# P in bursts of two key tiles, two head groups per PV bank, and another order of the prologue and the tail, in a post-LN transformer block

## The reference

```python
q, k, v = split(reshape(x @ qkv_w.T + qkv_b, heads), 3)
attn = softmax(q @ k.T * SCALE)
x = layernorm(x + (attn @ v) @ fc_w.T + fc_b + x)
h = silu(lin(x, w1, s1)) * lin(x, w2, s2)      # 128 -> 512
h = gelu(lin(h, h1)); h = gelu(lin(h, h2))     # 512 -> 512, exact gelu
x = layernorm(x + lin(h, w3))                  # 512 -> 128
```

## Time and profile before

| | before |
|---|---|
| median of 3 runs | 376.57 us (376.4 to 377.02) |
| profiled execution | 375.58 us, span 373.7 us |
| TensorE busy | 330.5 us (88%) |
| VectorE busy | 251.8 us (67%) |
| ScalarE busy | 249.3 us (67%) |
| GpSimd busy | 157.3 us (42%) |
| DMA | 13.30 MB, mean 36 GB/s |

### The profile page before, as it was taken

How to read it: one execution, slowest core, us unless ns; L and a number is a source line. 1 busy time by engine, 2 the same in 40 slices (tenths; PEclk the granted TensorE clock), 3 DMA queues, 4 the chain that set the end, 5 groups by cost and what they waited for, 6 DMA issues and landing times.

```text
span 373.7 us, 5421 instructions
## 1 busy us (share of the span) xinstructions
PE 330.5 (88%) x1712; PEld 156.5 (42%) x1738; DVE 251.8 (67%) x516; ACT 249.3 (67%) x441; POOL 157.3 (42%) x233
## 2 busy tenths in 40 slices
PE   2947999999999999999999899898997996887992
PEld 1611333222244343344544344363442352366891
DVE  4547878977789877679887678858365710044885
ACT  2605687777667786669667888849867778656440
POOL 9209483300018085004922186727438633308011
PEclk9985999999999999999999999999998998998997
DMA  4643404122130230211031102220000010000001
GB/s 100 191 93 66 150 3 71 38 43 39 16 65 0 36 52 1 44 26 18 3 71 21 25 11 35 43 59 1 0 2 1 1 31 0 1 2 0 2 28 32
DMA packets 21920, 13.30 MB, mean 36 GB/s; under 512 B 6787, under 2 KB 20739, under 8 KB 21891
## 3 DMA queue, kind: packets, MB, share of 16 engines
q1 hardware_dynamic: 21443, 12.53, 16.3%
q10 hardware_dynamic: 448, 0.39, 0.4%
HBM read 5.38 MB, written 1.05 MB: 17 GB/s over the span
## 4 chain that ended last, share of the span: by engine, by line
PE 70%; DVE 7%; ACT 7%; issue 7%; POOL 4%; ACTq 2%; DMA 1%; SPq 1%; POOLq 0%; another core or an unknown queue 0%; DVEq 0%
PE pv_bank L462 16%; PE f_bank L422 16%; PE s_bank L435 13%; PE st_bank L446 13%; DVE negmax L766 4%; ACT prob L628 3%; ACTq L338 2%; PE st_bank L422 2%; PE f_bank L483 2%; PE f_bank L405 2%; DMA res<-in_L_attn_fc_w_dram 1%; PE pv_bank L422 1%; POOL work L955 1%; PE s_bank L422 1%; ACT L628 1%
## 5 line engine op out<-in xcount | busy, mean ns | idle before, releaser
L766 DVE TENSOR_REDUCE negmax<-s_bank 128x1 f32<-128x512 f32 x256 | 167.8, 683 | 54.3 <-PE s_bank L435 52.3
L628 ACT ACTIVATE prob<-st_bank 128x512 f32<-128x512 f32 x256 | 142.0, 596 | 49.3 <-PE st_bank L446 41.4
L435 PE MATMUL s_bank<-stack 125*128 125x512 bf16 x256 | 96.9, 401 | 12.8 <-DVE negmax L766 5.9
L446 PE MATMUL st_bank<-stack 128*128 128x512 bf16 x230 | 82.7, 389 | 4.0 <-ACT prob L628 2.5
L462 PE MATMUL pv_bank<-prob,v_sb 128*32 128x512 f32 x512 | 73.2, 613 | 3.8 <-issue 3.6
L422 PE MATMUL f_bank<-act,hT 128*128 128x512 f32 (+1 forms) x224 | 70.2, 417 | 0.4 <-POOL act L965 0.4
L435 PEld LDWEIGHTS s_bank<-stack 125*128 125x128 bf16 x256 | 23.4, 98 | 78.2 <-DVE negmax L766 41.0
L446 PEld LDWEIGHTS st_bank<-stack 128*128 128x128 bf16 x256 | 23.9, 98 | 56.6 <-ACT prob L628 35.7
L422 PEld LDWEIGHTS f_bank<-act,hT 128*128 128x128 f32 x224 | 41.7, 191 | 8.6 <-issue 0.8
L931 POOL CAST mparts<-negmax 128x16 bf16<-128x16 f32 (+1 forms) x17 | 3.3, 196 | 88.4 <-DVE negmax L766 88.4
L977 POOL TENSOR_TENSOR act<-h_nat,act 128x512 fp32r<-128x512 f32 x24 | 30.4, 1273 | 1.3
(11 more groups left out here) (166 smaller groups left out, 411.2 us busy)
## 6 DMA issues: line engine op xcount, KB each, us to landing
stack<-parts SPq DMA_DIRECT2D x120, 48.0 KB
x_in<-in_L_attn_x_dram SPq DMA_DIRECT2D x4, 256.0 KB, 2.9
h_nat<-in_L_ffn_h_w_dram SPq DMA_DIRECT2D x1, 1024.0 KB, 6.6
work<-in_L_ffn_h_w_dram SPq DMA_DIRECT2D x1, 1024.0 KB, 5.9
x_res<-in_L_attn_x_dram SPq DMA_DIRECT2D x4, 256.0 KB, 2.9
out_dram<-y SPq DMA_DIRECT2D x3, 256.0 KB, 2.3
work<-in_L_ffn_w_w_dram SPq DMA_DIRECT2D x2, 256.0 KB, 5.0
stack<-parts ACTq DMA_DIRECT2D x8, 48.0 KB
```

Of the source, the lines that this page charges most:

```text
L435: nc.tensor.matmul(s_bank[n % NS][:, :], stack[0][0:MROW, h, qt * P:(qt + 1) * P], stack[1][0:MROW, h, :], start=True, stop=True).then_inc ...
L446: last = nc.tensor.matmul(st_bank[n % NST][:, to:to + nq], stack[1][:, h, kt * P:(kt + 1) * P], stack[0][:, h, q0:q0 + nq], start=True, st ...
L628: nc.scalar.activation(prob[:, n % NP, :], st_bank[n % NST][:, :], ACT.Exp, scale=SCALE).then_inc(ev_st, 1)
L766: nc.vector.tensor_reduce(negmax[:, g % 2, col:col + 1], s_bank[n % NS][:, :], AX.X, ALU.max, negate=True).then_inc(ev_s, 1)
```

## The change

- P: `PK = 2`. A P step covers two key tiles: eight matmuls (16 records) after eight T tiles, 34 steps instead of 68. `prob` has 12 slots.
- PV bank: heads are renumbered (`head_of`), V is stored as 18 columns per pair of places, 8 + 8 for two heads and one of ones each, and the P steps of two head groups accumulate in one `pv_bank`. `o`, `or` and `om` occur 8 times instead of 16. The V eviction is two instructions for the two places.
- Prologue: 28 products of zeros on TensorE (`keep_busy`), 22 before the first transpose and 6 after `wq`; the order of loads, transposes and splits is another; `vb` is loaded as one contiguous row to each partition, later; `db` moves from ScalarE to VectorE; the layer scales are loaded as rows and transposed (`hs`).
- `x_res` is `res[0]`; `xres` waits for `x1_ok` of the batch before.
- Tail: batch 2's second Gelu is applied at eviction (`direct`), its `gh` and `gl` move from GpSimd to VectorE; tables are loaded ahead with one-column activations (`ws`, `wg`); the last two units use `act1, act0, act1` where the others use `act0, act1, act0`, and their first split waits for the last H of batch 2 instead of its W.
- All five order texts are rewritten.

```diff
-    VW = 32
+    PO = 2
+    NO = NG // PO
+    VC, VW = PO * (HD + 1), 32
+    PK = 2
-    NP = 8
+    NP = 12
+    def head_of(s):
+        return GH * PO * (s // (GH * PO)) + PO * (s % GH) + s % (GH * PO) // GH
-        x_res = sb("x_res", [P, NT, D], F32)
+        x_res = res[0]
-        v_sb = [sb(f"v_sb{i}", [P, NT, H, VW], F32) for i in range(2)]
+        v_sb = [sb(f"v_sb{i}", [P, NT, H * VC + VW - VC], F32) for i in range(2)]
-        act2 = act0
+        acts = [(act0, act1, act0)] * LT + [(act1, act0, act1)] * TU
+        def direct(u, layer):
+            return u >= LT or (u, layer) == (LT - 1, 1) and True
...
+                elif what == "vb":
+                    sp.dma_start(vb[:, :], qkv_b.partition_broadcast(P)).then_inc(ld_vb, 16)
                 elif what == "xres":
-                    if n:
-                        until_empty(sp, "f", n - 1)
+                    sp.wait_ge(ps_wq, 2)
+                    wait(sp, x1_ok, n)
...
+            def keep_busy(times):
+                for _ in range(times):
+                    nc.tensor.matmul(pv_bank[:, 0:P], wz[:, :], wz[:, :], start=True, stop=True)
+            pe.wait_ge(wz_ok, 1)
+            keep_busy(22)
...
                 elif what == "P":
+                    g, first = n // (NT // PK), PK * n % NT
+                    b, s0, ns = GROUPS[g]
+                    t0 = P_LAST[n] + 1 - PK * ns
                     pe.wait_ge(ev_st, P_LAST[n] + 1)
+                    if first == 0:
+                        wait(pe, ev_pv, NO * b + s0 // (GH * PO))
+                        until_empty(pe, "v", b)
+                    for t in range(t0, t0 + PK * ns):
+                        _, kt, slot = T_TILES[t]
+                        at, of = VW * (slot % GH), VC * head_of(slot)
+                        last = nc.tensor.matmul(pv_bank[at:at + VW, :], v_sb[b % 2][:, kt, of:of + VW], prob[:, t % NP, :],
+                                                start=kt == 0 and slot % (GH * PO) < GH, stop=kt == NT - 1 and slot % (GH * PO) >= GH)
                     last.then_inc(ps_pv, 1)
...
+                elif what in ("ws", "wg"):
+                    nc.scalar.activation(warm[:, :], ident[:, 0:1], (ACT.Silu, ACT.Gelu)[what == "wg"])
...
-                        wait(dve, ps_w3, before(u))
-                    nc.vector.tensor_copy(act0[0][:, k, cols(u)], gate[:, k, cols(u)]).then_inc(hi0 if u < LT else hi0_t, 1)
+                        dve.wait_ge(*((ps_w3, u) if u < LT else (ps_h, 2 * NK * LT)))
+                    nc.vector.tensor_copy(acts[u][0][0][:, k, cols(u)], gate[:, k, cols(u)]).then_inc(hi0 if u < LT else hi0_t, 1)
```

The order texts, their first lines and the parts that matter (a stretch without feed-forward work, and the end of TensorE's and ScalarE's lists):

```diff
 SP_ORDER
-xin lw lh xin zq*2 zk*2 zq zk*2 zq*3 mrow zq*2 lh l3 mrow*2 more xres spread mrow xin spread mrow spread mrow spread mrow xres spread mrow spread mrow
+lw lh xin vb zq*5 zk lh zq zk zq*2 mrow zk*2 l3 xin mrow xin mrow more xres spread mrow spread mrow spread mrow spread xres mrow spread mrow spread
 PE_ORDER
-x:0 wq wf q:1 q:2 v:5 x:0 wt:6 wt:7 v:1 wt:5 wt:2 wt:6 wt:0 S*11 m:1 S*5 T S T S*2 T S P m:2 S*2 T*2 q:0 S*2 P S T*2 q:1 S P S T*2 S wt:2 P S T S T
+x:0 wq wt:1 q:2 q:5 wt:6 v:7 wf wt:0 wt:1 wt:2 wt:5 x:0 v:1 S*11 m:0 S*7 wt:6 S wt:7 S m:1 T*2 S wt:2 S T wt:0 S T S T q:1 S*2 P S*2 T*2 q:2 S T*2 S
...
-S P S*2 T*2 S T S T P S*2 T*2 o:1 S T S T P S a:0 S T S m:2 T f:1 S*2 T*2 P S T*2 q:0 T S T P S T q:2 S T*2 S v:1 S x:0 T S T P T*2 X:2 o:0 S T*2 P S
+T*2 S T S T*2 S T S P S*2 T*2 S T S T m:0 T S T S T S*2 P S*2 T*2 S T S T*2 S T S T S T S T*2 S P S*2 m:2 T*2 S T S T S T*2 S*2 T*2 P S*2 T*2 o:1 S T
...
-T P T*2 H T*2 P T*2 H H:0 T H T H*2 T H:2 T H*2 T H T H:1 H*3 P*2 T o:0 T*3 P T*4 P T*2 H:2 H*2 P H H:1 o:0 H*2 a:3 a:4 H f:5 H:6 H*3 H:7 H*3 f:2 X:0
-A:3 B:4 A:1 B:5 A:6 B:7 A:2 B:0 X:3 W:1 A:4 B:6 A:5 B:2 A:7 W B:3 A:0 B:4 W*2 H:5672 Y:3 H*9 H:0415 H*9 H:6723 H*9 H:0415 H*9 W:6 W*3 W:7 Y:2 W*3 Y:3
+T*2 m:0 Y:2 T*2 P T*2 H:1 o:2 T H T*3 H T*2 P T*2 H H:0 T*2 H*2 T H T H:2 T H T P T*2 H*2 T*2 H:1 H T H T H T P T*7 P o:0 H:2 a:1 a:3 H f:4 H*2 H:5
+H*3 H:6 H X:7 f:0 H*2 H:1 H*3 A:3 B:4 A:2 B:5 W:0 W*2 X:6 W A:7 B:1 A:3 B:2 Y:4 A:0 B:6 A:7 B:5 A:3 B:1 A:0 B:2 H:7360 H*9 H:5127 H*9 H:3604 H*9
 ACT_ORDER
-t e*2 u e*3 o e*2 h e*2 h t h*2 g u e*4 m e*2 t e*4 o w3 e*7 m e*7 h e*2 h e*2 h*2 g o e*12 o h a*2 h*3 g t*8 w3 h*16 w3*2
+m o e*10 h e*3 h e*5 h e*4 h g e*8 wg o a*2 h*4 ws t*2 w3 t*6 wg h*16 w3*2
```

More of the change, by code:

```diff
@@ L8 @@
 SP_ORDER = """
-xin lw lh xin zq*2 zk*2 zq zk*2 zq*3 mrow zq*2 lh l3 mrow*2 more xres spread mrow xin spread mrow spread mrow spread mrow xres spread mrow spread mrow
-spread mrow spread mrow spread xres mrow spread mrow spread mrow spread out xres mrow*3 out*4
+lw lh xin vb zq*5 zk lh zq zk zq*2 mrow zk*2 l3 xin mrow xin mrow more xres spread mrow spread mrow spread mrow spread xres mrow spread mrow spread
+mrow spread mrow spread mrow xres spread mrow spread mrow spread mrow spread out xres mrow*3 out*4
@@ L494, in step @@
                     rows = m_rows(n)
-                    for t in range(m_tiles(n)):
-                        last = nc.tensor.transpose(space("m", n)[:, :].bitcast(BF16)[0:rows, t * P:(t + 1) * P],
-                                                   mparts[:, t * rows:(t + 1) * rows], ident16[:, :])
-                    last.then_inc(ps_mT, 1)
+                    nc.tensor.transpose(space("m", n)[:, :].bitcast(BF16)[0:rows, 0:P], mparts[:, 0:rows], ident16[:, :]).then_inc(ps_mT, 1)
                 elif what == "o":
@@ L588, in step @@
                     last.then_inc(ps_wt, 1)
+                elif what == "hs":
+                    pe.wait_ge(ld_s, 16 * 5)
+                    until_free(pe, "hs", 0)
+                    nc.tensor.transpose(space("hs", 0)[:, 0:4 * NK + 1], hs_nat, ident[0:4 * NK + 1, 0:4 * NK + 1]).then_inc(ps_hs, 1)
                 elif what == "L":
@@ L733, in layernorm @@
                     dve.wait_ge(ps_w3T, u + 1)
+                    wait(dve, y_ok, before(u))
                     nc.vector.tensor_tensor(flat(r), space("Y", u)[:, 0:width(u)], flat(x1_b), ALU.add).then_inc(emptied("Y", u), 1)
```

243 lines of the change are left out of this document (120 added, 123 removed).

## The result

The changed kernel takes 373.56 us (median of 20 runs, 369.84 to 377.01), the kernel before 375.7 beside it (20 runs); the ratio is 0.9921, interval 0.9892 to 0.9951. The forecast was 363.0 with a range of 355.5 to 371.5, so the time is above the range. The profiled execution took 373.0 us, span 371.2, against 375.58 and 373.7: 2.5 us less on the span, where the sum had 13.6.

What follows compares the result with a forecast made beforehand. TensorE was taken as full where feed-forward work runs, a loop of latencies as binding elsewhere; -4.4 - 2.2 - 3.0 + 1.0 - 1.0 - 4.0 = -13.6 us off the 376.57 median gave 363.0 us, range 355.5 to 371.5.

Steps and rivals of the forecast that it cites:

- Bursts, -4.4: P steps: joining 68 into 34 saves 0.20 us at each of 22 pairs where TensorE is full, 4.4 us.
- pairs, -2.2: PV bank: two head groups per bank drop eight times four transposes; five in full stretches at 0.43 save 2.2 us.
- Prologue, -3.0: Start: earlier q, faster clock by fillers and reordered work bring the first S to 20 to 21.5; 3.0 us gained.
- xres, +1.0: Group changes: xres waits for x1_ok, so the next mrow and T may come late; 1.0 us lost in all.
- Wide Gelu, -1.0: Stall of 3.61 us before the P at 314.65: remains, with eight exponentials after it instead of twelve; 1.0 us gained.
- Tail, -4.0: End: direct Gelu, early table loads and exchanged buffers cut last P to first tail H from 21.0 to about 17; 4.0 gained.
- from there on nothing changes: After the first tail H: 128 tail matmuls without gaps, normalization and store stay as before.
- One sign: Tail, expected in the new profile: no table load between the last H and the first gate.
- Rival (a): Full stretches: half of 6.6 us is given back and the tail gains 1.5 only; -7.8, 368.8 us, chance 0.25.
- The hand-worked round: Loop stage without feed-forward work: eight tiles take 6.8 us with a burst against 6.7 now, so 0 booked.
- Rival (c): All 34 bursts: the longer pause is covered nowhere, 0.9 less 0.2 us each, +24; 391 us, chance 0.05.
- rival (d): All bursts: rival (c)'s mechanism at 0.3, so no change; 376.6 us, chance 0.03.

Runs made afterwards that it cites:

- e15: The changed kernel with both the max reductions and the exp activations halved (wrong results); 356.8 us, 0.9528 of the kernel before.
- e16: The kernel before with both the max reductions and the exp activations halved (wrong results); 367.59 us, 0.9817 of the kernel before.
- e14: The kernel before with the paired PV banks alone, eight evictions instead of sixteen; 374.72 us, 1.0004 of the kernel before.
- e13: The changed kernel with one head group per PV bank, sixteen evictions instead of eight; 388.16 us, 1.0345 of the kernel before.
- e3: The changed kernel without the 28 filler products; 372.37 us, 0.9917 of the kernel before.
- e2: The kernel before with its P steps joined in pairs and 12 prob slots, nothing else; 383.8 us, 1.0224 of the kernel before.
- e9: The kernel before with its max reductions halved and the exp scale reduced (wrong results); 371.73 us, 0.9929 of the kernel before.
- e11: The kernel before with its exp activations halved (wrong results); 370.9 us, 0.9868 of the kernel before.
- e18: The changed kernel's code with the old loop and old TensorE prologue order, keeping pairs, fillers and new tail with mended VectorE order; 371.3 us, 0.987 of the kernel before.

## Why the prediction failed, step by step

**Bursts, -4.4, and pairs, -2.2: together +0.7 in the loop.** This is the step that cost most. Both counts were right (34 bursts, 1.92 us; eight evictions, below), the work came off, and the assumption failed that in a full stretch work taken off TensorE is time. I had read "TensorE is full" off a sum of 38.1 to 40.3 of 40 us, the size of the uncertainty being as large as the saving; counted by intervals, the stretch had 2 to 3 us of gaps and the next ones 3 to 5. The evidence against was already in the prediction: in the loop stage it worked out that eight tiles take 6.8 us with a burst and 6.7 without, and booked 0; that the same limit holds with H pieces between is what e15 and e16 show. And the pairs were priced by their transposes (5 x 0.43). What they are worth is the eviction's place behind a burst:

```profile
L663 ACT ACTIVATE oT<-pv_bank 128x512 f32<-128x512 f32 x8 | 4.8, 595 | 11.4 <-PE pv_bank L472 11.4
```

1.4 us of standing for each, where it was 0.4. Two edits that were summed are one: without bursts 0 (e14), with them up to 13 us of the loop (e13).

**Prologue, -3.0: -2.4 at the first S, -2.2 at P64, part of it luck.** The way was another than told: q starts at 8.53 instead of near 8.0, since the transposes ahead of it wait 1.41 us for w, and not all of it runs at the upper level; the fillers are worth nothing (e3). And the number hangs on which execution was profiled. In six profiles with the old order of the prologue's loads and transposes, TensorE's clock rises to its upper level at 12.2 to 12.4 us (e2, e9, e16) or at 14.2 to 14.6 (before, e11, e14); V's projection then takes 1.05 us or 1.79 to 1.91, and the first S starts at 21.5 to 21.8 or at 23.7 to 24.0 (V's projection in before, then in e2):

```profile
12.71 1.79 PE L488 MATMUL st_bank<-qkvT,xT 128*128 128x128 f32 x8
```

```profile
12.54 1.05 PE L488 MATMUL st_bank<-qkvT,xT 128*128 128x128 f32 x8
```

The kernel before was profiled with the late rise; against the early one the changed kernel's 21.30 is 0.2 to 0.5 us ahead, and its own prologue gives 20.72 to 22.73 over twelve profiles. The lead at the first S is also not carried on: the first exp starts at 37.3 us in both. Kernels with the old order and a first S at 21.4 to 21.8 (e2, e9, e16, e18) have it at 33.9 to 34.2. The new order has twenty S ahead of the first T, the old one sixteen, and four tiles at 0.7 us are most of that difference.

**xres, +1.0: 0.** No T waits for a row of maxima in the changed kernel.

**Wide Gelu, -1.0: no gain that shows.** Between 300 and 320 us, where the earlier trace rows lies, the gaps are 6.2 us after 6.7, but between 220 and 260 they are 6.5 after 4.0: one of the other wide Gelus, with two table loads (224.55 to 229.05), now meets a stretch without feed-forward work, S at VectorE's pace, T waits, and the clock falls to the lower level for 3.4 us from 229.2.

```profile
228.55 0.39 PE L447 MATMUL s_bank<-stack 125*128 125x512 bf16 x1 [0.21 <-DVE negmax L781]
229.71 0.61 PE L457 MATMUL st_bank<-stack 128*128 128x512 bf16 x1 [0.77 <-DVE negmax L781]
...
231.96 2.20 PE L472 MATMUL pv_bank<-prob,v_sb 128*32 128x512 f32 x16
```

**Tail, -4.0: -3.8 up to the first tail H, then +2.7.** For the earlier trace rows:

```profile
321.55 3.48 PE L472 MATMUL pv_bank<-prob,v_sb 128*32 128x512 f32 x16 [0.69 <-ACT prob L639]
...
342.20 0.28 PE L434 MATMUL pv_bank<-act,hT 128*128 128x256 f32 x1
```

From the end of the last P (325.0) it is 17.2 us to the first tail H, 21.0 before; "about 17" was forecast. The step that failed is "from there on nothing changes": VectorE's entries after it had been reordered, and I didn't go through them. One sign was missed: a table load does stand between the last H (335.61) and the first gate, and the gate's matmul, done by 336.5, waits for it. It costs nothing that shows, since TensorE has work without a break until the first tail H:

```profile
336.74 1.28 ACT L669 ACT_TABLE_LOAD   x1
338.04 0.20 ACT L669 ACTIVATE warm<-ident 128x1 f32<-128x1 f32 x1
338.15 0.46 ACT L685 ACTIVATE work<-s_bank,hs_all 128x256 f32<-128x256 f32 x1
```

The sum as measured: -2.2 + 0.7 - 1.0 = -2.5 us on the span. Rival (a) had the mechanism, "the pauses leave VectorE and ScalarE behind and the full stretches get gaps", at half its size; in full (6.6 us given back, the tail at -1.0) it gives 13.6 - 6.6 - 3.0 = 4.0 us gained, 372.6 us. I held against it that both engines have a third of their time free, the argument that e15 refutes. The hand-worked round said that a burst gains nothing, and should have gone into every stretch. (Rival (c) breaks even at 9.2/34 = 0.27 us per burst; at the 0.3 of rival (d) it gives 377.6, not 376.6.)

## What to carry to other kernels

A share of 88% is no proof that an engine sets the time: where three engines pass tiles over two banks each, take the round, not the sum. Work taken off in exchange for a longer pause must be priced by what the paused engines then catch up at, and an instruction that stands behind the pause in their queue by the whole pause; edits that meet in such a place are to be priced together. In a changed static order, walk every engine's list to the end: 2.7 us lay in the part where "nothing changes".

## What the runs showed of the hardware that I had not expected

The changed kernel's single executions differ by 7 us, and they go with the mean granted clock: 369.8 us at 0.957, 373.0 at 0.947, 377.0 at 0.930, while the kernel before stays between 373.2 and 377.0, and at 0.948 to 0.963 in the runs beside the experiments. The latter's spread is mostly not the clock's mean: 373.3 and 376.6 both ran at 0.962. In the profiled one the clock stands at its lower level for 6.8 us from 317.9, and the last burst pays for it: 3.48 us instead of 1.92. The low stretch at the start is longer too, 17.1 us from 21.0 against 13.7 from 24.5, with the fillers and without. It isn't what keeps the first exp at 37.3 us: e18 has 17.1 us of it too, and the old order, and its first exp starts at 34.2. That pauses of TensorE bring such stretches is what the rows suggest (one begins at the end of the wide Gelu's stall above); no run here tests it by itself.

A subtraction of VectorE over 512 columns (L780) takes 0.68 us in most rows and 0.78 to 1.65 us in others. In each of the slow rows of before and e2 a GpSimd instruction over 512 columns was already running when it began, and the subtraction ended 0.53 to 0.55 us after that one did: 1.65 us at 17.27, beside GpSimd's 17.04 to 18.37; 1.01 at 44.47, beside 44.33 to 44.95; 1.08 at 15.95 in e2, beside 15.88 to 16.48. Where GpSimd's instruction began after it, it took 0.68 (15.81, beside 16.07 to 16.96).
